# A mixed graph network in float32: the first weighing step written as two halves of 256 columns

## The reference

```
h = jnp.maximum(_layernorm(x, axis=-1), 0.0)
x = x + _L0_gnn_ref(h, adj, ...)
...
x = x + _L3_gnn_ref(h, adj, ...)
```

## Time and profile before

| | us |
|---|---|
| median of 3 runs | 1376.95 |
| the three runs | 1377.80, 1374.58, 1376.95 |
| span of the profiled execution, first to last instruction (its time as a run is not listed apart) | 1374.0 |
| TensorE busy (matmul) | 1334.7 |
| VectorE busy | 1238.5 |
| ScalarE busy | 1000.8 |
| GpSimd busy | 996.9 |

### The profile page before, as it was taken

One profiled execution on the slowest core, in us unless ns is written; L12 is line 12 of the kernel. 1 busy time (PEld: TensorE's weight loads), 2 busy tenths in 40 slices (PEclk: granted clock), 3 DMA queues, 4 the chain that ended last, 5 costly groups with the idle time before them and its releaser, 6 DMA issues.

```text
span 1374.0 us, 32347 instructions
## 1 busy us (share of the span) xinstructions
PE 1334.7 (97%) x10772; PEld 1289.6 (94%) x10772; DVE 1238.5 (90%) x3863; ACT 1000.8 (73%) x2376; POOL 996.9 (73%) x2005
## 2 busy tenths in 40 slices
PE   4899999999999999999999999999999999999996
PEld 3799999999999999999999999999999999999985
DVE  5799999999999999999999999999999999999974
ACT  3677777777777777777777777777777777777763
POOL 4677777777777777777777777777777777777741
PEclk8999999999999999999999999999999999999999
DMA  7011111111112112111111111101111111111000
GB/s 195 23 33 55 41 43 55 44 40 55 48 36 55 48 36 55 47 36 55 48 36 55 50 33 55 56 28 55 55 32 51 55 32 51 55 32 36 29 9 24
DMA packets 83220, 64.49 MB, mean 47 GB/s; under 512 B 40304, under 2 KB 65520, under 8 KB 83056
## 3 DMA queue, kind: packets, MB, share of 16 engines
q1 hardware_dynamic: 83056, 62.43, 16.2%
HBM read 45.62 MB, written 16.78 MB: 45 GB/s over the span
## 4 chain that ended last, share of the span: by engine, by line
PE 93%; DVE 2%; POOL 1%; ACT 1%; SPq 1%; issue 1%; DMA 1%; DVEq 0%; POOLq 0%
PE BANK L323 30%; PE BANK L291 24%; PE BANK L330 15%; PE WIDE L323 8%; PE WIDE L302 8%; PE WIDE L330 4%; PE BANK L341 2%; PE BANK L276 2%; DMA X_B<-in_xs 1%; SPq L226 0%; DVE BN_C L497 0%; ACT H_D L370 0%; DVE BN_B L497 0%; DVE Z_B L585 0%; ACT UHI_D L401 0%
## 5 line engine op out<-in xcount | busy, mean ns | idle before, releaser
L401 ACT ACTIVATE UHI_B<-BANK 128x512 fp32r<-128x512 f32 x96 | 57.3, 597 | 46.2 <-PE BANK L291 46.2
L401 ACT ACTIVATE UHI_C<-BANK 128x512 fp32r<-128x512 f32 x96 | 57.3, 596 | 43.8 <-PE BANK L291 43.8
L401 ACT ACTIVATE UHI_D<-BANK 128x512 fp32r<-128x512 f32 x96 | 57.3, 597 | 43.1 <-PE BANK L291 42.8
L401 ACT ACTIVATE UHI_A<-BANK 128x512 fp32r<-128x512 f32 x96 | 57.3, 597 | 43.1 <-PE BANK L291 43.1
L538 DVE TENSOR_TENSOR ULO_D<-BANK,UHI_D 128x512 fp32r<-128x512 f32 x96 | 64.6, 673 | 16.1 <-ACT UHI_D L401 16.1
L538 DVE TENSOR_TENSOR ULO_B<-BANK,UHI_B 128x512 fp32r<-128x512 f32 x96 | 64.6, 673 | 11.2 <-ACT UHI_B L401 11.2
L538 DVE TENSOR_TENSOR ULO_C<-BANK,UHI_C 128x512 fp32r<-128x512 f32 x96 | 64.6, 673 | 10.9 <-ACT UHI_C L401 10.9
L538 DVE TENSOR_TENSOR ULO_A<-BANK,UHI_A 128x512 fp32r<-128x512 f32 x96 | 64.7, 674 | 10.0 <-ACT UHI_A L401 10.0
L673 POOL TENSOR_TENSOR LN_B<-LN_B,MHALF 128x2 f32<-128x2 f32 x80 | 55.9, 699 | 1.3
L673 POOL TENSOR_TENSOR LN_D<-LN_D,MHALF 128x2 f32<-128x2 f32 x80 | 55.5, 694 | 1.3
L673 POOL TENSOR_TENSOR LN_A<-LN_A,MHALF 128x2 f32<-128x2 f32 x80 | 55.5, 694 | 1.3
(11 more groups left out here) (486 smaller groups left out, 5728.2 us busy)
## 6 DMA issues: line engine op xcount, KB each, us to landing
X_A<-in_xs SPq DMA_DIRECT2D x16, 256.0 KB, 3.0
X_B<-in_xs SPq DMA_DIRECT2D x16, 256.0 KB, 2.9
X_C<-in_xs SPq DMA_DIRECT2D x16, 256.0 KB, 2.9
X_D<-in_xs SPq DMA_DIRECT2D x16, 256.0 KB, 2.8
out_rows<-O_A SPq DMA_DIRECT2D x16, 256.0 KB, 2.0
out_rows<-O_B SPq DMA_DIRECT2D x16, 256.0 KB, 2.1
out_rows<-O_C SPq DMA_DIRECT2D x16, 256.0 KB, 2.0
out_rows<-O_D SPq DMA_DIRECT2D x16, 256.0 KB, 2.1
```

Of the source, the lines that this page charges most:

```text
L401: nc.scalar.activation(UHI[s][:, 0:J * D], bank(s, step, k)[:, :], ACT.Copy).then_inc(sem(f"c{step}"), 1)
```

## The change

In `weigh`, for the step `0W` alone, the loop over j becomes a loop over the pairs (j, half). A half is 256 of the 512 output columns: `dst` is that half of the bank, and the moving operand is the matching half of the weights. All three products of a half are done, from the start flag to the stop flag, before the next half begins. The wait for `l0U` stands ahead of the low-part matmuls of the first half of the first j. The signal `p0W` comes after the second half of each j. The other weighing steps are as they were.

```
-                    for j in range(J):
-                        dst = to[:, j, :] if step == "0W" else to[:, j * n:(j + 1) * n]
+                    parts = [(j, half) for j in range(J) for half in range(2 if step == "0W" else 1)]
+                    for j, half in parts:
+                        cut = slice(half * D, (half + 1) * D)
+                        dst = to[:, j, cut] if step == "0W" else to[:, j * n:(j + 1) * n]
                         at = [j * chunks * P + m * P for m in range(chunks)]
...
                         for w in (lo, hi):
                             for m in range(chunks):
-                                nc.tensor.matmul(dst, UHI[s][:, at[m]:at[m] + P], w[:, m, :],
+                                nc.tensor.matmul(dst, UHI[s][:, at[m]:at[m] + P], w[:, m, cut],
                                                  start=(w is lo and m == 0), stop=False)
...
-                        elif j == 0:
+                        elif j == 0 and half == 0:
                             pe.wait_ge(sem(f"l{step[0]}U"), c["n1"])
                         for m in range(chunks):
-                            last = nc.tensor.matmul(dst, ULO[s][:, at[m]:at[m] + P], hi[:, m, :], start=False,
+                            last = nc.tensor.matmul(dst, ULO[s][:, at[m]:at[m] + P], hi[:, m, cut], start=False,
                                                     stop=(m == chunks - 1))
-                        if step == "0W" or j == J - 1:
+                        if half == 1 or step != "0W" and j == J - 1:
                             last.then_inc(sem(f"p{step}"), 1)
```

## The result

The changed kernel takes 1394.42 us (median of 4 runs, 1392.82 to 1395.17) beside 1375.76 us for the kernel before on the same chip: a ratio of 1.0133, 95% interval 1.0119 to 1.0146. It is slower, by 18.7 us; the forecast was 8.3 us slower, and the time lies above the range. The profiled execution took 1393.7 us, of which 1391.9 us are the span.

A forecast was written before the change was run, and what follows sets the result against it. TensorE, without slack, was taken to bound the kernel; the early wait's 4.1 + 2.0 + 1.8 + 0.4 = +8.3 us on 1376.95 gave 1385.2 us, range 1378 to 1389.5.

The forecast's parts named there:

- What bounds the kernel: Steady stretch, 100 to 1240 us: TensorE busy 1139.99 of 1140.00 us, so a pitch change or new wait counts at full size.
- The moved wait: In 0W, before the first low-part matmuls: TensorE waits 0.135 us in an ordinary turn; step +0.095 us, +8.3 us in all.
- The wait persists in every turn: ULO ahead of 0W: its end stays 9.83 us after 6U whatever the period, so the wait comes every turn.
- the rival in which it is relieved: GpSimd's pass shifts ahead of VectorE's Z_B, ULO comes earlier, 0W's wait goes: -4.3 us, 1372.7 us; chance 0.08.
- The new matmuls by themselves: In 0W, 24 matmuls of 256 columns for 12 of 512: -0.07 to +0.02 us a step, -4.5 to +1.3 over 64.
- the slow pitch behind the wait: Rival in 0W: the wait falls and 117.5 ns a matmul holds behind it; 2.955 us a step, +12.0 us, 1389.0; chance 0.12.
- The signs of being wrong: 0W at 2.73 us with the next pair at 0.70 us, or a turn longer by less than 0W is.
- The fixed cost per matmul of the Trainium skill: In 0W: N/2.4 + 2.5 ns a warm matmul, so 12 more cost 30 ns a step, 1.9 us in all.

## Why the prediction was wrong

**What bounds the kernel**: right. TensorE has no slack in the steady stretch, and what a turn grew by, 17.6 us in 64 turns, is nearly all of the total.

**The moved wait**: right in place, limit and size. It said that the pair behind the low part can't start earlier than 0.40 us after ULO's end; in the 54 steady steps that were read it starts 0.39 to 0.41 us after it. It said that ULO ends 9.83 us after 6U whatever the period; in the turn above it is 9.81 (181.85 less 172.04), and its mean from 100 to 1225 us is 9.91 before and 9.92 after. 0W was to take 2.895 us in an ordinary turn and +8.3 us in all; its mean is 2.925, and 0.129 x 64 = 8.3 us. That the sum agrees to a tenth is in part luck: ULO's end is 0.02 us nearer to the start on the mean than before (0.457 for 0.474), because it comes at 0.39 in 18 steps, and the 18 matmuls behind the wait take 0.02 us more than forecast (2.072 for 2.055). The run with halves and a late wait shows that this loss is the early wait's, on balance. The wait persists in every turn, as argued; the rival in which it is relieved did not come.

**The new matmuls by themselves**: here it failed. What failed is the term for the pitch, taken over 0W alone, so that the other steps of the turn stood at nothing without a reason. The step priced the pitch of 256 columns at 114 to 117.5 ns and applied both prices to 0W only, "Pitch alone is thus worth between -0.07 and +0.02 us a step". Inside 0W that nearly holds: without the early wait its steps take 2.72 or 2.83 us for 2.80. It read two rows with two pitches for the same instruction, took them as the bounds of an unknown price, and did not ask what decides between them. It is a state that one step hands to the next. The 512 columns at the end of 0W were what set it for 5W, 2W and 3W, and in part for 6W and 1W behind them: 72 matmuls of that kind a turn outside 0W. The missing term is 0.145 us a turn, 9.3 us, larger than the one that was found. The sentence that the steps other than 0W stay as they were was nowhere written, and for that reason nowhere questioned; a turn "grows by about 0.1 us" rests on it. The signs of being wrong had a turn that grows by less than 0W, but none that grows by more, as it did: 0.275 us for 0W's 0.129.

**The rivals**: the nearest was the slow pitch behind the wait, +12 us, which kept to 0W as well. The 2.88 to 2.96 us that the prediction gave for 0W held in the mean (single steps lie from 2.83 to 3.19); what it gave as the total did not. The fixed cost per matmul of the Trainium skill (TensorE: Matmul & The Clock Gate, Back-to-back issue gap) would have added 1.9 us; the run with halves and a late wait has 12 matmuls more in 0W at the same mean of 2.80 us, so no run here bears it out.

## What to carry to other kernels

Where the trace before shows two prices for one and the same instruction, find out which neighbour decides between them before you choose one: the answer may lie in another step and carry the change's larger half. On a queue without idle time, compare all steps of a turn, not the edited one alone; a shift of 4% in the pitch of untouched matmuls was as dear here as the wait. And where a group of matmuls is cut smaller, count again how much work still stands ahead of each wait: cut in half, the cover is halved too.

## What was not expected of the hardware

Matmuls of 256 columns on this split-operand path stand either 113.5 or 117.6 ns apart, at the same granted clock of 1.00. The state lasts through plain float32 steps, whose own pace is the same in both kernels (110 ns a matmul on the mean in the steps of line 291), and through the first 512-column pair of 0W. Behind float32 steps it depends on how the matmuls ahead of them ended. For 0W, 5U and 5W: after 512 columns 5W is quick in 321 of 330 turns and after 384 in all 55; after 256 it is slow unless the last of them stands 120 ns ahead of 5U. 4W shows the like in the kernel before: 1W ends quick in 53 of 55 turns, and 4W begins slow in 52 of these; in the two turns with a slow 1W, 4W is quick. What it is in the machine, no run here tells.

Matmuls of 512 columns stand 231 and 236 ns apart in turn, 467 ns a pair, which lies between four of 256 at the quick pitch (454 ns) and four at the slow one (470 ns). The saving that this suggests was had in one step of four in the run with halves and a late wait (2.72 us in 14 of 54); the others began in the slow pitch that 4W leaves.
